# A state's product with B, made by GpSimd instead of VectorE beside the experts

## The reference

```python
def step(state, xs):
    d_t, B_t, C_t, u_t = xs
    dA = jnp.exp(d_t[..., None] * A)
    state = state * dA + (d_t * u_t)[..., None] * B_t[:, None, :]
    y_t = jnp.einsum('ben,bn->be', state, C_t)
    return (state, y_t)
...
output = _expert_ffn(x, Ws1, Wsg, Ws2)
...
for e in range(NUM_ROUTED):
    w_e = jnp.sum(topk_probas * (topk_idxs == e), axis=-1)
    output = output + _expert_ffn(x, W1[e], Wg[e], W2[e]) * w_e[..., None]
```

## Time and profile before

| | |
|---|---|
| median of 3 runs | 1540.28 us (1538.64 to 1541.5) |
| the profiled execution | 1539.44 us |
| its span, first to last instruction | 1537.3 us |
| mean granted TensorE clock | 0.933 |
| instructions | 18479 |

### The profile page before, as it was taken

One profiled execution on the slowest core, in us unless ns is written; L12 is line 12 of the kernel. 1 busy time (PEld: TensorE's weight loads), 2 busy tenths in 40 slices (PEclk: granted clock), 3 DMA queues, 4 the chain that ended last, 5 costly groups with the idle time before them and its releaser, 6 DMA issues.

```text
span 1537.3 us, 18479 instructions
## 1 busy us (share of the span) xinstructions
PE 1369.0 (89%) x6183; PEld 1071.7 (70%) x6183; DVE 1092.0 (71%) x1323; ACT 473.2 (31%) x795; POOL 453.9 (30%) x240
## 2 busy tenths in 40 slices
PE   8555459999999996999999986999999999999999
PEld 4333337777777774787777864787777878888887
DVE  5899985799998965579999955579999962322222
ACT  3633214644343312432223212433223211111111
POOL 3200004477777730022233310023233311111111
PEclk9687569999999997999999997999999999999999
DMA  6111272676665554365555564365555564665552
GB/s 204 38 55 54 93 263 112 221 257 236 235 230 207 202 211 173 111 213 177 163 169 175 168 224 139 117 210 178 166 167 177 166 220 136 215 210 193 195 169 82
DMA packets 90806, 266.43 MB, mean 173 GB/s; under 512 B 11472, under 2 KB 11600, under 8 KB 90336
## 3 DMA queue, kind: packets, MB, share of 16 engines
q1 hardware_dynamic: 85472, 258.39, 49.5%
q10 hardware_dynamic: 5248, 6.96, 1.3%
HBM read 207.39 MB, written 57.93 MB: 173 GB/s over the span
## 4 chain that ended last, share of the span: by engine, by line
PE 67%; DVE 22%; issue 6%; ACT 2%; DMA 2%; SPq 1%; DVEq 0%; ACTq 0%; POOL 0%
PE ps_hg L452 19%; PE ps_h L452 18%; PE ps_y L452 12%; DVE st L1059 10%; PE ps_y L591 8%; DVE y_rows L1065 5%; PE ps_mid L517 4%; DVE st L1050 3%; PE ps_mid L499 1%; PE ps_mid L495 1%; PE ps_mid L492 1%; DMA st<-xin_scratch 1%; DVE h_tmp L1174 1%; DVE h_tmp L1179 1%; DMA w_raw<-in_Ws_dram 1%
## 5 line engine op out<-in xcount | busy, mean ns | idle before, releaser
L1312 POOL TENSOR_TENSOR h_lo<-h_tmp,h_hi 128x512 fp32r<-128x512 f32 x128 | 280.8, 2193 | 799.3 <-ACT h_hi L827 799.3
L452 PE MATMUL ps_h<-x_hi,w_split 128*128 128x512 f32 x1024 | 352.5, 406 | 7.0 <-DVE x_lo L1106 4.3
L452 PE MATMUL ps_hg<-x_hi,wg_split 128*128 128x512 f32 x1024 | 348.8, 402 | 0.0
L1059 DVE TENSOR_TENSOR_SCAN st<-dA,st 128x1024 f32<-128x1024 f32 x128 | 298.2, 2330 | 0.0
L517 PE MATMUL ps_mid<-ident,st 128*128 128x128 f32 x1024 | 173.8, 300 | 94.0 <-DVE st L1059 49.6
L452 PE MATMUL ps_y<-w_split,h_hi 128*128 128x512 f32 x1024 | 256.4, 398 | 0.8 <-ACT h_hi L827 0.8
L517 PEld LDWEIGHTS ps_mid<-ident,st 128*128 128x128 f32 x1024 | 132.5, 153 | 153.8 <-DVE st L1059 92.4
L452 PEld LDWEIGHTS ps_h<-x_hi,w_split 128*128 128x128 f32 x1024 | 196.3, 192 | 49.4 <-issue 4.9
L452 PEld LDWEIGHTS ps_hg<-x_hi,wg_split 128*128 128x128 f32 x1024 | 194.7, 190 | 40.8 <-issue 0.3
L1174 DVE SCALAR_TENSOR_TENSOR h_tmp<-h_tmp,ps_h 128x512 f32<-128x512 f32 x128 | 87.8, 686 | 183.2 <-ACT h_tmp L821 182.5
L452 PEld LDWEIGHTS ps_y<-w_split,h_hi 128*128 128x128 f32 x1024 | 189.0, 189 | 39.6 <-ACT h_hi L827 2.0
(11 more groups left out here) (122 smaller groups left out, 1018.1 us busy)
## 6 DMA issues: line engine op xcount, KB each, us to landing
w_split<-split_scratch SPq DMA_DIRECT2D x192, 512.0 KB, 4.8
wg_split<-split_scratch SPq DMA_DIRECT2D x96, 512.0 KB, 4.2
split_scratch<-w_split SPq DMA_DIRECT2D x64, 512.0 KB, 4.2
b_all<-xd_scratch SPq DMA_DIRECT2D x64, 256.0 KB, 3.8
split_scratch<-wg_split SPq DMA_DIRECT2D x32, 512.0 KB, 3.1
w_raw<-in_W_dram SPq DMA_DIRECT2D x14, 1024.0 KB, 7.8
wg_raw<-in_Wg_dram SPq DMA_DIRECT2D x7, 1024.0 KB, 10.0
dA<-in_x_dram SPq DMA_DIRECT2D x4, 1024.0 KB, 8.5
```

What stands on the lines that cost most here:

```text
L452: mm = pe.matmul(out_, lhs[a], rhs[c], start=first and q == 0, stop=last and q == len(sides) - 1)
L1059: dve.tensor_tensor_scan(flat[1], flat[0], flat[1], 0.0, ALU.mult, ALU.add).then_inc(scan_done, 1)
L1312: pool.tensor_tensor(h_lo[:, j, :], h_tmp[j % 2][:], h_hi[:, j, :].bitcast(F32), ALU.subtract).then_inc(hl_ready, 1)
```

## The change

The states of sequence 0 keep their bmul on VectorE. In the three batches beside the experts, GpSimd makes it: B(0, 0) and B(0, 1) in the step e = 1 behind h_lo of tile 3 (and its split), and in each state step, with `first` = a: both halves of a ahead of the step's first h_lo, both halves of a + 1 behind h_lo of tile 1 (behind U2 in batch 0), B(a + 2, 0) ahead of h_lo of tile 3, and B(a + 2, 1) at the end. The waits for b_all, u and the transposes of n - 2 go with it. GpSimd's loop over the experts of batches 1 and 2 is written out.

```diff
@@ VectorE, slot @@
-                if n < DS:
-                    (bmul if r % 2 == 0 else scan)(m, n, r // 2)
+                if n < DS and r % 2:
+                    scan(m, n, r // 2)
+                elif n < DS and not some(m):
+                    bmul(n, r // 2)
@@ GpSimd @@
+            def bmul(m, n, h):
+
+                odd = n % 2
+                two = slice(2 * h, 2 * h + 2)
+                if h == 0:
+                    pool.wait_ge(bc_ld[odd], 16 * (DS // RING * m + n // RING + 1))
+                    pool.wait_ge(du_ready, m + 1)
+                    if n >= 2:
+                        bank, before = mid(m, sum_place(n - 2, T - 1))
+                        pool.wait_ge(mid_done[bank], before + 1)
+                    if n == 1:
+                        pool.wait_ge(coef_ready, 2 * m)
+                pool.tensor_tensor(st[odd][:, two], u[:, two],
+                                   b_all[odd][:].rearrange("p (a l) -> p a l", a=1).broadcast_to([P, 2, L]),
+                                   ALU.mult).then_inc(bmul_done, 1)
...
+            def state_step(step, m, first, split):
+                for h in range(2):
+                    bmul(m, first, h)
+                for j in range(T):
+                    if split:
+                        split_up(step + 1, j)
+                    if j == 2:
+                        for h in range(2):
+                            bmul(m, first + 1, h)
+                    if j == 3:
+                        bmul(m, first + 2, 0)
+                    h_low(step, j)
+                    if split:
+                        split_gate(step + 1, j)
+                bmul(m, first + 2, 1)
+                if split:
+                    split_down(step + 1)
...
-                if split:
-                    for e in range(1, NE):
-                        step_(STEPS * b + e, split)
-                else:
-                    with pool.Fori(1, NE) as e:
-                        step_(STEPS * b + e)
+                step_(STEPS * b + 1, split, first_routed)
+                for e in range(2, NE):
+                    state_step(STEPS * b + e, m, 3 * (e - 2) + 1, split)
```

More of the change, by code:

```diff
@@ L1041, in front_du, with bmul @@
                                          op0=ALU.mult, op1=ALU.mult).then_inc(du_ready, 1)
-            def bmul(m, n, h):
-                N, odd = DS * m + n, n % 2
+            def bmul(n, h):
+                odd = n % 2
                 two = slice(2 * h, 2 * h + 2)
                 if h == 0:
-                    dve.wait_ge(bc_ld[odd], 16 * (DS // RING * m + n // RING + 1))
-                    dve.wait_ge(du_ready, m + 1)
+                    dve.wait_ge(bc_ld[odd], 16 * (n // RING + 1))
+                    dve.wait_ge(du_ready, 1)
                 dve.tensor_tensor(st[odd][:, two], u[:, two],
@@ L1214, in _ @@
             front_du(0)
-            bmul(0, 0, 0)
-            bmul(0, 0, 1)
+            bmul(0, 0)
+            bmul(0, 1)
             front_z2(0, (0, 1))
@@ L1336, in step_, with first_routed @@
                     split_down(step + 1)
+            def state_step(step, m, first, split):
[15 more added lines that the diff above has]
+                    split_down(step + 1)
             def batch(b, m):
                 split = isinstance(b, int) and b == 0
+                def first_routed(j):
+                    if j == 3:
+                        for h in range(2):
+                            bmul(m, 0, h)
                 step_(STEPS * b, split, lambda j: power(zvar, zrstd, m) if j == 1 else None)
-                if split:
-                    for e in range(1, NE):
-                        step_(STEPS * b + e, split)
-                else:
-                    with pool.Fori(1, NE) as e:
-                        step_(STEPS * b + e)
+                step_(STEPS * b + 1, split, first_routed)
+                for e in range(2, NE):
+                    state_step(STEPS * b + e, m, 3 * (e - 2) + 1, split)
                 step_(STEPS * b + NE)
```

## The result

The changed kernel takes **1584.76 us** (1582.99 to 1587.85) against 1540.82 before, a ratio of 1.029 (1.0268 to 1.0311): 44 us slower, where 58 were forecast. The span of the profiled execution went from 1537.3 to 1581.6 us, 44.3 more.

The account below looks back on a forecast made before the run. The SBUF port shared by VectorE and GpSimd was to decide, filling batch 0's steps; TensorE's floor was 38.6 us a step. Terms 34 + 18 + 5 = 57 on 1539.4, median offset 0.8, clock 1: 1598 us, range 1572 to 1620.

Parts of the forecast that it names:

- The port: VectorE instructions reading two SBUF tensors (scan, bmul) and GpSimd ones exclude each other whole; whoever waits goes next.
- The price of B: One 128x1024 product on GpSimd: 2.4 us, with 2.3 to 2.55 likely.
- Batches 1 and 2: State steps: products hold scans, 41.8 us against 39.95, +1.85 each, +1.45 in e = 6; +18 in all.
- Batch 0: State steps: 47.9 us of port work plus 2.5 free makes 50.5, +6.85 each, five times: +34.
- The e = 1 steps: Tail of three e = 1 steps: first products hold scans, 1.2 in batches 1 and 2, about 2.6 in batch 0: +5.
- The floor: TensorE's work in a state step, products, transposes and down matmuls: 38.6 us.
- rival A: The relief wins: no exclusion, or B short, from 1.7 us down; 1502, with half of it 1520; 4%.
- The clock: TensorE's waits may lower its granted clock: 0 to 1.6 us in each of ten steps; 1 us added.
- The signs to look for: Profile after: GpSimd busy up well over 230 us, B 4.6 behind a scan, scan mean over 2.33, TensorE's waits grown.
- B (a draw): Batches 1 and 2 reach most of the floor and pay for batch 0; needs B near 1.7; 3%.
- C (only batch 0 pays): In batches 1 and 2 scans come early enough to miss B; 34 + 3 to 5: 1577; 18%.
- E (more): B at 2.55 or above, and TensorE's clock falls in most of ten steps (+16): 1607 to 1625; 20%.

Follow-up runs that it names:

- the scans beside a memset: Changed kernel's GpSimd product kept in batch 0 only and replaced there by a constant memset of the same 1024 columns: 1521.51 us, ratio 0.9884 to the kernel before.
- halved products: Changed kernel's GpSimd products kept in batch 0 only, each covering 512 of 1024 columns: 1535.89 us, ratio 0.9977 to the kernel before.
- the run with batches 1 and 2 alone: GpSimd makes the product with B only in batches 1 and 2, VectorE keeps it in batch 0: 1557.33 us, ratio 1.0112 to the kernel before.
- B at 1.25: Changed kernel with every GpSimd product with B halved to 512 columns, in all three batches: 1534.31 us, ratio 0.9961 to the kernel before.
- the run with the other order: Changed kernel, but in batches 1 and 2 B(a+2,0) stands behind h_lo3 instead of ahead: 1598.53 us, ratio 1.0377 to the kernel before.
- the last kernel with a product in batch 0: Kernel before with only B(a+1,1) on GpSimd, behind h_lo2, in batches 0 to 2, and batch 0's later splits moved behind h_lo3: 1534.01 us, ratio 0.9952.

## Why the prediction was right, and where its sizes were off

The total was 1598, and 1584.76 were measured: inside the range of 1572 to 1620, but under the stretch that was called most likely, 1587 to 1607. The direction and the mechanism were right. The 13.7 us too many are four terms, all too high: about 8 in batch 0, 2.4 in batches 1 and 2, 2.3 in the e = 1 steps and 1 for the clock.

**The port.** Right, and shown twice: the held scans of the changed kernel, and the scans beside a memset that aren't held. The rule cited from the Trainium skill (SBUF — State Buffer, Who interferes with whom), that a VectorE instruction with two SBUF inputs contends with a GpSimd one that reads SBUF and not with one that only writes, agrees with 4.24 against 2.28 us beside a product and 2.28 beside a memset.

**The price of B.** Right: 2.40 us alone, 4.76 for two in a row, against 2.4 forecast. The estimate from the Trainium skill's GPSIMD Engine Reference (section 3.1), 2.25, was 0.15 low. The mean in the trace, 2.60, includes the time held.

**Batches 1 and 2.** The mechanism was right place by place: scan(a+1,0) held 0.75 (forecast 0.95), h1(3) 0.77 later through the decay (25.30 us after up0 begins, 24.53 before), scan(a+1,1) held 1.96 (1.95). The step came to 41.54 against 41.8; +1.6 in place of +1.85, and +1.36 in e = 6 in place of 1.45.

**Batch 0.** Right in kind, 27.7 us of forecast 34 plus 2.6. The term that was mis-sized is the step of 50.5 us: it measured 48.2 to 49.8, mean 48.9, over a base of 43.35 and not 43.65. I had it as 47.9 us of port work and 2.5 us free. In the trace of the changed kernel, the scans, products, splits and h_lo of a step laid over each other cover 45.7 to 46.9 us in the last four steps, mean 46.3, and leave 2.5 to 2.9 free, mean 2.7. (The first window, with the two products of e = 1 in it as well, is covered for 48.1 of its 48.2 us.) So the free time was about right, and the port's work was 1.6 us too high: behind one another the instructions take up less than the sum of the durations I gave them, as B(a,0) and B(a,1) in 4.76 and not 4.80, and a scan held by a product ends 2.15 after it and an h_lo held by a scan 1.1 after that. The work before is 38.9 by the same count, in steps of 43.35.

In the layout GpSimd took B(a+2,0) ahead of scan(a+1,1). In the trace that hangs on 0.2 us and goes either way:

```profile
404.35 2.38 POOL L1341 TENSOR_TENSOR st<-u,b_all 128x1024 f32<-128x1024 f32 x1
...
453.72 4.24 POOL L1341 TENSOR_TENSOR st<-u,b_all 128x1024 f32<-128x1024 f32 x1 [0.57 <-PE ps_mid L517]
```

```profile
404.56 4.31 DVE L1059 TENSOR_TENSOR_SCAN st<-dA,st 128x1024 f32<-128x1024 f32 x1
...
453.49 2.28 DVE L1059 TENSOR_TENSOR_SCAN st<-dA,st 128x1024 f32<-128x1024 f32 x1
```

The steps with the product first took 48.2 and 49.2, those with the scan first 49.0, 49.8 and 48.2: the order did not make the difference. With halved products, 40.9 us of work by count of durations and 40.0 by the trace, the steps took 42.6.

**The e = 1 steps.** Forecast +5; cut at the first add, e = 1 itself moved by 0.2 us or less, and the window behind it, which has its tail and most of e = 2, paid 0.5 more than its neighbours in batches 1 and 2 (2.14 against 1.62) and about 1.7 more in batch 0: 2.7. (Cut at the last add, as the earlier trace rows has batch 0, the tail counts for e = 1: 3.6 more in batch 0 and 2.0 in each of the others, and the five steps behind take less.) scan(0,0) was held there as forecast (4.37 us), but TensorE's waits for scans in that window of batch 2 sum to 2.4 us against 1.7 in the next steps, so 0.7 more where I had 1.2.

**The floor.** 38.6 us a step was too low. The shortest steps e = 3 to 5 in batches 1 and 2 measured, with one wait of 0.6, are 39.5, of which TensorE is busy 38.91. (No run has such a step without a wait, so the floor itself was not measured.) Little hung on it here, since nothing was won; in rival A it would have cut the gain of batches 1 and 2 to about a third.

**The clock.** I added 1 us for it. In these steps of batches 1 and 2 of the changed kernel it stayed at 1.00 and cost nothing; TensorE's longest wait there is 1.1 us, and its waits sum to 2.5 us a step (forecast 2.7). In batch 0 it fell to 0.90 to 0.97. TensorE waits 7.7 us a step there, where I had over 10, 4.6 at most where I had about 5. What the lower clock cost in batch 0 was not separated: the longest step, 49.8, is also the one at 0.90.

**The signs to look for.** B at 2.4 alone and at most 4.39 behind a scan (4.6 forecast), scans 2.86 us in the mean, TensorE's waits for y_rows 78.4 us against 43.5: seen. Its waits for scans hardly grew, 51.5 against 49.6. GpSimd's busy time grew by 220, not by "well over 230", partly since its h_lo were held less (2042 ns against 2193).

**Rivals.** A (the relief wins) is out: it needed B below 1.7 us, and with B at 1.25 the whole program is 6 us faster than before, so its condition was about right and its price of 38 was not. B (a draw) is out with it, since it needed the same B. C (only batch 0 pays) is out by the run with batches 1 and 2 alone, +18 us. E (more) is out: B took 2.40, and the clock stayed at 1.00 in the ten steps.

## What to carry to other kernels

Idle time of GpSimd is not room for work that reads SBUF while VectorE has instructions with two SBUF inputs: add up what both hold, per stage. Where the sum passes the stage's length, as in batch 0, the stage grows to the sum and a little more (here 46.3 us covered in steps of 49).

Where it fits, place decides. In batches 1 and 2 the six products bring the covered time of a step from 25.1 to only 31.7 us, in steps of 40, and still cost 1.6 us each step, 18 us in all; one product in the gap between two scans, taken off the chain, won 3.6 us in the same batches. So a sum that fits settles nothing: the places must be followed one by one, and an order that frees one scan can hold the next two.

## What the runs showed that I had not expected

The granted clock fell in steps whose longest wait was 2.0 us. In the five windows of batches 1 and 2, the changed kernel's longest wait of TensorE was 1.1 us, and the clock kept 1.00. In the run with the other order it was 2.0 us in the windows of e = 3 to 6 of batch 2. Three of these four show 0.96, and the two of them among e = 3 to 5 last 1.5 to 1.6 us more than the one at 1.00 between them. Batch 0 of the kernel before, with waits up to 2.3, shows the same mixture. The longest wait alone doesn't settle it: in the last kernel with a product in batch 0, two neighbouring steps, both with a longest wait of 2.2 us and 3.8 or 3.9 us in all, show 1.00 and 0.96, the second 1.6 us longer. What exactly makes the clock fall was not tried.

A memset of 1024 columns on GpSimd takes 0.94 to 0.97 us in all 32 cases, whether a scan begins beside it or not: in these runs writing doesn't meet the scan at all.
